# Attention block on one core: the last stage moved into the attention loop, two token tiles to a job, inverse root on GpSimd

## What is computed

```python
h = layernorm(x) * (1 + ca) + sa
q, k, v = split(h @ W_attn)                      # 16 heads of 16
att = softmax(causal(q @ k.T / 4)) * decay       # decay is 0 beyond 512 tokens back
x = x + ga * ((att @ v) @ W_proj)
h = layernorm(x) * (1 + cb) + sb
x = x + gb * (h @ (W + lora_weight).T + b)
```

## Time and profile before

| | |
|---|---|
| median of 3 runs | 1557.8 us (1557.61 to 1559.09) |
| profiled execution | 1560.7 us, its span 1558.8 us |
| mean granted TensorE clock | 0.966 of 2.4 GHz |
| busy over the span | PE 1280.6, ACT 1311.0, DVE 996.6, POOL 52.4 us |
| attention, first product to last rescaling | 205.9 to 1471.2 us |
| last stage, first load to the end of the span | 1474.7 to 1558.8 us |

### The profile page before, as it was taken

The page is one execution under the profiler, slowest core; times in us unless marked ns, Lnnn a source line. Parts: engine busy times, 40 slices in busy tenths (PEclk is TensorE's granted clock), DMA queues, the critical chain, the costliest instruction groups (busy, mean ns, idle before and its releaser), DMA issues. The chain is left out here.

```text
span 1558.8 us, 28424 instructions
## 1 busy us (share of the span) xinstructions
PE 1280.6 (82%) x11067; PEld 737.5 (47%) x11067; DVE 996.6 (64%) x2026; ACT 1311.0 (84%) x2677; POOL 52.4 (3%) x28
## 2 busy tenths in 40 slices
PE   7876168888888888888888888888888888777598
PEld 5543034545454545444445444554544444333387
DVE  4632147777777777777777777777776666554376
ACT  2533069999999999999999999999999999999532
POOL 0322000000000000000000000000000000000022
PEclk9988579999999999999999999999999999999799
DMA  4999970101010101010100000000101000100153
GB/s 149 203 218 198 169 97 1 35 1 35 2 35 1 35 1 29 7 35 2 27 10 17 20 13 23 11 26 8 25 6 27 9 23 10 23 4 4 37 168 128
DMA packets 111723, 72.96 MB, mean 47 GB/s; under 512 B 56395, under 2 KB 110946, under 8 KB 111586
## 3 DMA queue, kind: packets, MB, share of 16 engines
q1 hardware_dynamic: 111586, 71.13, 21.3%
HBM read 45.93 MB, written 25.17 MB: 46 GB/s over the span
## 5 line engine op out<-in xcount | busy, mean ns | idle before, releaser
L808 PE MATMUL fast_s_ps<-k_stack,fast_q_stack 96*128 96x512 bf16 (+3 forms) x2448 | 651.9, 354 | 178.2 <-ACT fast_probs L927 98.7
L927 ACT ACTIVATE fast_s_ps<-fast_s_ps,fast_negmax 128x1024 f32<-128x1024 f32 (+4 forms) x768 | 792.8, 1039 | 4.4 <-PE fast_s_ps L808 3.9
L949 DVE TENSOR_REDUCE fast_negmax<-fast_s_ps 128x1 f32<-128x640 f32 (+4 forms) x512 | 399.1, 780 | 134.5 <-PE fast_s_ps L811 130.0
L927 ACT ACTIVATE fast_probs<-fast_s_ps,fast_negmax 128x640 f32<-128x640 f32 (+7 forms) x512 | 436.6, 853 | 43.3 <-DVE fast_negmax L949 38.7
L958 DVE TENSOR_TENSOR fast_probsT<-fast_t_ps,fast_dec_c 128x384 f32<-128x384 f32 (+2 forms) x512 | 276.6, 540 | 197.1 <-PE fast_t_ps L826 197.1
L808 PEld LDWEIGHTS fast_s_ps<-k_stack,fast_q_stack 96*128 96x128 bf16 x2448 | 180.0, 97 | 451.2 <-ACT fast_s_ps L927 178.0
L826 PE MATMUL fast_t_ps<-ident,fast_probs 128*128 128x128 f32 x1488 | 250.2, 275 | 22.7 <-DVE fast_y_sb L989 20.8
L968 DVE TENSOR_TENSOR fast_probsT<-fast_t_ps,fast_dec_c 128x256 f32<-128x256 f32 x464 | 191.6, 413 | 66.9 <-PE fast_t_ps L842 66.9
L826 PEld LDWEIGHTS fast_t_ps<-ident,fast_probs 128*128 128x128 f32 x1488 | 172.4, 141 | 76.2 <-DVE fast_y_sb L989 27.9
L842 PE MATMUL fast_t_ps<-ident,fast_probs 128*128 128x128 f32 x912 | 187.2, 286 | 1.9
L857 PE MATMUL fast_t_ps<-fast_probsT,fast_vals 128*16 128x128 f32 x4800 | 180.9, 276 | 7.1 <-DVE fast_probsT L968 5.9
(11 more groups left out here) (107 smaller groups left out, 588.1 us busy)
## 6 DMA issues: line engine op xcount, KB each, us to landing
parts_d<-part SPq DMA_DIRECT2D x48, 256.0 KB, 12.5
k_stack<-parts_d SPq DMA_DIRECT2D x48, 256.0 KB, 9.7
fast_q_stack<-parts_d SPq DMA_DIRECT2D x192, 64.0 KB, 3.0
fast_vals<-v_d SPq DMA_DIRECT2D x36, 128.0 KB, 3.0
xs<-x_dram SPq DMA_DIRECT2D x8, 512.0 KB, 8.6
v_d<-w SPq DMA_DIRECT2D x8, 512.0 KB, 8.6
y_d<-fast_y_sb SPq DMA_DIRECT2D x32, 128.0 KB, 2.5
yy<-y_d SPq DMA_DIRECT2D x16, 256.0 KB, 2.7
```

The source lines that it names most:

```text
L808: last = nc.tensor.matmul(s_ps[:, n % SLOTS, o:o + w], q, k_stack[:, h, P * b0 + o:P * b0 + o + w], start=True, stop=not diag)
L927: nc.scalar.activation(dst, src, ACT.Exp, bias=negmax[:, p % 2, side, h:h + 1], scale=-1.0, accum_out=sums[:, p % 2, side, h, c:c + 1]).th ...
L949: nc.vector.tensor_reduce(out=negmax[:, p % 2, side, h:h + 1], in_=s_ps[:, n % SLOTS, max(0, cols - P * WIN):cols], axis=AX_X, op=ALU.min) ...
```

## The change

The last stage is taken out of its place behind the attention (it stays as `rest_full`, called only behind `attention_full`) and is done inside `attention_fast`, pair by pair. Both tiles of a finished pair make one job of 512 columns on bank two of `t_ps`, behind FAR's turn in steps h = 5 (turn of y), 7 (product with `wp_g`), 11 (turn of the normalised rows) and 13 (product with `wf_g`) of the next pair; for the last pair they follow behind the loop. In such steps fill 4 stands ahead of FAR's tail, as it did in group steps. VectorE takes over ScalarE's two copies; row statistics come in h = 8, the aggregates in h = 9. GpSimd computes 1/sqrt(var + eps) with an integer first guess and four Newton steps, 11 small operations a tile, each waiting for the one before, then normalises and adds the bias. q is loaded in halves of 8 heads, and y no longer goes to HBM.

```diff
+            HEAD_JOBS = {1: ("back", FAR), 3: ("back", NEAR)}
+            BOTH = 2
+            TAIL_JOBS = {5: ("y_turn", BOTH), 7: ("project", BOTH), 11: ("n_turn", BOTH), 13: ("linear", BOTH)}
...
-                q_stack = sb("fast_q_stack", [SROWS, 2, 2, NH, P], bf16, s2)
+                q_stack = sb("fast_q_stack", [SROWS, 2, 2, QH, P], bf16, s2)
...
+                    for u in range(2 * NPAIR):
+                        p = u // 2
+                        if u + 2 < 2 * NPAIR:
+                            sp.wait_ge(s_full, PER * QH * (u + 1))
+                            load_q(u + 2)
+                        if u % 2 == 0 and 0 < p < NPAIR - 1:
+                            sp.wait_ge(tail_full, tail_no["group", NEAR, NG4 * p - 1] + 1)
+                            load_vals(p + 1)
+                        if u % 2 == 1 and p > 0:
+                            store(p - 1)
+                            if p + 1 < NPAIR:
+                                sp.wait_ge(result_stored[(p - 1) % 2], 32 * ((p - 1) // 2 + 1))
+                                load_x(p + 1)
...
+                    def y_turn(p):
+                        pe.wait_ge(tail_free, tail_no["y_turn", BOTH, p])
+                        pe.wait_ge(turn_free, turn_no["back", NEAR, p] + 1)
+                        for side in (FAR, NEAR):
+                            for cc in range(CH):
+                                o = P * (CH * side + cc)
+                                last = nc.tensor.transpose(tail_ps[:, o:o + P], y_sb[:, side, P * cc:P * (cc + 1)], ident[:])
+                        last.then_inc(tail_full, 1)
+                    def through(weights, job):
+                        pe.wait_ge(tail_free, tail_no[job])
+                        for side in (FAR, NEAR):
+                            for cc in range(CH):
+                                last = nc.tensor.matmul(tail_ps[:, C * side:C * (side + 1)], tT[:, side, cc, :], weights[:, cc, :],
+                                                        start=(cc == 0), stop=(cc == CH - 1))
+                        last.then_inc(tail_full, 1)
+                    def n_turn(p):
+                        pe.wait_ge(norm_ready, 2 * p + 2)
...
                         turn(FAR, s)
                         if group_after(s):
                             values(*group_after(s), 1)
+                            fill(s, 4)
+                            turn_tail(FAR, s)
+                        elif job_after(s, TAIL_JOBS):
+                            tail_job(*job_after(s, TAIL_JOBS))
                             fill(s, 4)
                             turn_tail(FAR, s)
...
+                    def inverse_root(side):
+                        v, half, y, w = (b[:, side:side + 1] for b in (var_e, var_h, rstd, root_t))
+                        chained(nc.gpsimd.tensor_scalar(v, mv2[:, side, 1:2], EPS, None, ALU.add))
+                        chained(nc.gpsimd.tensor_scalar(half, v, -0.5, None, ALU.mult))
+                        chained(nc.gpsimd.tensor_scalar(y.bitcast(mybir.dt.int32), v.bitcast(mybir.dt.int32),
+                                                        -0.5, 1597463007.0, ALU.mult, ALU.add))
+                        for _ in range(4):
+                            chained(nc.gpsimd.tensor_scalar(w, y, y, half, ALU.mult, ALU.mult))
+                            chained(nc.gpsimd.tensor_scalar(y, w, three_halves[:, 0:1], y, ALU.add, ALU.mult))
+                    for p in range(NPAIR):
+                        for side in (FAR, NEAR):
+                            pool.wait_ge(stats_done, 2 * p + side + 1)
+                            inverse_root(side)
+                            x2 = xb[:, p % 2, side, :]
+                            nc.gpsimd.tensor_scalar(y_sb[:, side, :], x2, mv2[:, side, 0:1], rstd[:, side:side + 1],
+                                                    ALU.subtract, ALU.mult).then_inc(norm_ready, 1)
+                            pool.wait_ge(norm_ready, 2 * p + side + 1)
+                            nc.gpsimd.tensor_tensor(x2, x2, f_bias[:], ALU.add).then_inc(bias_added, 1)
...
+                    def row_sums(h, p):
+                        if h == 8:
+                            spread(FAR, p)
+                            spread(NEAR, p)
+                        if h == 9:
+                            statistics(FAR, p)
+                            statistics(NEAR, p)
```

More of the change, by code:

```diff
@@ L710, in attention_fast @@
                 next_tail("group", side, NSTEP // HG - 1)
-            for side in (FAR, NEAR):
-                next_turn("back", side, NPAIR - 1)
+            for kind, side in HEAD_JOBS.values():
+                next_turn(kind, side, NPAIR - 1)
+            for kind, side in TAIL_JOBS.values():
+                next_tail(kind, side, NPAIR - 1)
             s2 = ExitStack()
@@ L761, in _, with load_q @@
                 def _(sp):
-                    def load(p):
+                    def load_q(u):
+                        p, half = u // 2, u % 2
                         for side in (FAR, NEAR):
@@ L774, in store @@
                     def store(p):
                         for side in (FAR, NEAR):
[L776 to L784, removed]
-                            sp.wait_ge(tail_full, tail_no["group", NEAR, NG4 * p - 1] + 1)
-                            load(p + 1)
-                        store(p - 1)
+                            sp.wait_ge(tail_free, tail_no["linear", BOTH, p] + 1)
@@ L869, in turn_back, with head_job, tail_job @@
                         last.then_inc(turn_full, 1)
+                    def y_turn(p):
[15 more added lines that the diff above has]
+                        pe.wait_ge(norm_ready, 2 * p + 2)
+                        pe.wait_ge(tail_free, tail_no["n_turn", BOTH, p])
+                        for side in (FAR, NEAR):
+                            for cc in range(CH):
+                                o = P * (CH * side + cc)
+                                last = nc.tensor.transpose(tail_ps[:, o:o + P], y_sb[:, side, P * cc:P * (cc + 1)], ident[:])
+                        last.then_inc(tail_full, 1)
+                    def head_job(kind, side, p):
+                        turn_back(side, p)
+                    def tail_job(kind, side, p):
+                        if kind == "y_turn":
+                            y_turn(p)
+                        elif kind == "project":
+                            through(wp_g, (kind, side, p))
+                        elif kind == "n_turn":
+                            n_turn(p)
+                        else:
+                            through(wf_g, (kind, side, p))
                     pe.wait_ge(k_last, 16 * len(PAIRS))
@@ new lines, in result, with head_job @@
+                    def result(p):
+                        dve.wait_ge(tail_full, tail_no["linear", BOTH, p] + 1)
+                        dve.wait_ge(bias_added, 2 * p + 2)
+                        x2 = xb[:, p % 2]
+                        nc.vector.tensor_tensor(x2, x2, tail_ps.rearrange("p (s c) -> p s c", s=2), ALU.add).then_inc(tail_free, 1)
+                    def head_job(kind, side, p):
+                        if side == FAR:
+                            factors(p)
+                        finish(side, p)
@@ L1015, in _ @@
                     group_to_sb(NEAR, NSTEP // HG - 1)
-                    factors(NPAIR - 1)
-                    finish(NPAIR - 1, FAR)
-                    finish(NPAIR - 1, NEAR)
+                    for h in range(NH):
+                        row_sums(h, NPAIR - 1)
+                        if h in HEAD_JOBS:
+                            head_job(*HEAD_JOBS[h], NPAIR - 1)
+                        if h in TAIL_JOBS:
+                            tail_job(*TAIL_JOBS[h], NPAIR - 1)
                     nc.vector.tensor_reduce(out=worst_row[:], in_=worst[:], axis=mybir.AxisListType.XY, op=ALU.max
@@ L1660 @@
+            rest_full()
 def kernel(**inputs):
```

527 lines of the change are left out of this document (298 added, 229 removed).

## The result

The changed kernel takes **1618.4 us** (median of 4 runs, 1617.07 to 1621.29), the kernel before 1558.4 (4 runs, 1557.61 to 1568.1): ratio 1.0373, 95% interval 1.0329 to 1.0416. It is slower by 3.7%; the forecast was 1545.8 with a range to 1581, so the time lies outside it. The cause is rival A, larger than I had priced it.

The account below looks back on a forecast made before the run. ScalarE's exponentials were taken to bound the attention (97% busy). From a span of 1558.8 us, 59.2 saved at the end, 50.6 given back inside the attention and 3.4 saved at the start made 12.0 less: 1545.8 us, range 1526 to 1581.

Parts of the forecast that it names:

- rival A: GpSimd late for the turn of n at h = 11, TensorE and ScalarE waiting: 1582 us at c = 0.45; chance 0.20.
- GpSimd's chain: Inverse root, normalisation and bias of both tiles, between h = 9 and 11: 9.0 us in 9.7 available, cost 0.
- T: Time of GpSimd's work on a pair's two tiles, 22c + 0.5 + 0.75 + 0.5 + 0.2, predicted 9.0 us.
- c: Time of one small chained GpSimd operation: taken as 0.32 us between bounds 0.24 and 0.40; stops fitting at 0.355.
- Large jobs: Product and add in h = 7 and 13 of 15 pairs: each step loses 1.41 us on average.
- Rival B: Jobs in the attention better hidden by ScalarE's three slots: 21 us given back instead of 50.6, 1516 us; chance 0.13.
- Small jobs: Turn and copy in h = 5 and 11 of 15 pairs: each step loses 0.28 us on average.
- Rival C: Delay carries into the even step behind each job: 60 x 0.42 = 25 us more, 1571 us; chance 0.11.
- Row statistics: VectorE's statistics in h = 8 and h = 9 fall into its idle time: 0; without that cover up to 12 us.
- The start: Loading q in halves starts the attention's first product earlier: 3.4 us saved, bounds 0 and 9.
- The old stage's clock: The stage behind the attention, 87.6 us removed, was said to run its 16 batches of 4.33 us at full clock.
- The end: Last pair's jobs run alone after the last rescaling, ending at 1499.6 instead of 1558.8: 59.2 us saved.

Follow-up runs that it names:

- experiment 6: Changed kernel with the inverse root for both tiles at once, no pointer operands, still four Newton steps, 19 operations instead of 22: 1554.0 us, ratio 0.9943 to the kernel before.
- experiment 1: Changed kernel with two Newton steps on GpSimd instead of four: 1558.4 us, ratio 0.9974 to the kernel before.
- experiment 5: Changed kernel with 20 throwaway transposes on TensorE ahead of its wait for the normalised rows, in all pairs but the last: 1598.7 us, ratio 1.0235.
- experiment 3: Changed kernel with the turn of the normalised rows at h = 13 and the product behind it at h = 15: 1558.75 us, ratio 0.9970.
- experiment 10: Kernel before with q loaded in halves of eight heads and nothing else of the change: 1558.5 us, ratio 0.9961.
- experiment 7: Changed kernel with the inverse root moved to VectorE in h = 9, normalisation and bias staying on GpSimd: 1648.1 us, ratio 1.0548.
- experiment 2: Changed kernel with three Newton steps on GpSimd instead of four: 1571.4 us, ratio 1.0041 to the kernel before.
- experiment 4: Changed kernel with the turn of the normalised rows at h = 13 and six Newton steps instead of four: 1562.4 us, ratio 0.9995.

## Why the prediction was wrong

- **GpSimd's chain, the step that failed.** The rule was right: late by T less 9.7. T was mis-sized: 22c + 0.5 + 0.75 + 0.5 + 0.2 = 9.0, measured 12.4. Of the 3.4 us, 2 x 0.75 = 1.5 are the normalisation (0.5 taken, 1.25 measured), which I had costed as "one input less" and not bounded at all; 22 x (0.41 - 0.32) = 1.9 are the small operations. c lay just over the upper bound of 0.40, because of the pointers (experiment 6), which the prediction named as absent from every row of before and then left outside the bound. The normalisation itself, same size and same two pointers, did stand in the trace of before, on VectorE (L1646): 0.41 us, the median of 32 (experiment 6). The prediction did not use it. With 1.25 for each normalisation c would have had to stay under (9.7 - 3.45) / 22 = 0.284. The choice "T = 9.0 fits: 0" with 0.7 us to spare between bounds 3.5 us apart (22 x 0.16) was no forecast to give 0.56 to. The Trainium skill (GPSIMD Engine Reference, section 4.1) says that on GpSimd an operation with one input is "roughly line-rate" against VectorE; the trace does not bear this out for this form: the 128x256 one with one tensor input and two pointers takes 1.22 to 1.25 us on GpSimd, three times its 0.41 on VectorE, and more than GpSimd's two-input one of the same size (0.72).
- **Rival A's price.** With the measured T it gives 1546.8 + 15 x 2.65 + 3.4 = 1590 us of span; the span is 1617.4, 27 more. In the steps GpSimd's lateness costs 60 us (experiment 1) where this formula has 15 x 2.65 = 40; the clock, with 22 us in pairs 1 to 14 (experiment 5), more than fills that gap of 20. The rest is 3.5 for the jobs (54.1 against 50.6), the drain's other 1.8, and 1.3 in h = 3 of pair 13, where the clock fell too. The low clock stood in the rows, at the seam, where I used it for the drain; I did not ask what a wait of TensorE inside the attention would do to it.
- **Duration and spacing.** The Trainium skill (Perfetto Trace Analysis, GPSIMD Engine Instruction) advises timing GpSimd by start-to-start spacing. The trace agrees: a pointer operation shows 344 ns, and the next, which waits for it, starts 444 ns after it did.
- **Large jobs: right.** 1.41 us predicted, 1.41 measured at h = 7 and 13; by pair 1.34 in pair 1 (1.3 predicted), 1.60 in pair 7 (1.6), 1.82 in pair 15 (1.8). Counting through the step's chain, tried on the turning back at h = 3, holds. Rival B falls.
- **Small jobs:** 0.28 predicted, 0.14 measured (h = 5, and h = 13 in experiment 3: 0.15).
- **Rival C:** a carry-over into the next even step exists, at 0.09 to 0.12 us in h = 6, 8 and 14, not 0.42.
- **Row statistics,** costed at nothing: h = 9 is unchanged and h = 8 0.09 longer, in which the carry-over of h = 7 lies as well. Right.
- **The start:** 3.4 predicted, 3.1 measured in this profile; by experiment 10 closer to 6. Inside its bounds of 0 and 9.
- **The old stage's clock.** The prediction has its batches "all at full clock"; the clock was 0.50 until 1484, so the first product took 3.82 us. The 87.6 us removed do not rest on this.
- **The end:** 28.4 us predicted from the last rescaling, 33.5 measured: 3.4 are GpSimd's, and behind the result's add it is 7.2 against 5.4; what the stores take there I had read off the old stage's single one. To the start of GpSimd (7.5) and from the turn of n to the result (6.4) it is as predicted.

With T under 9.7 the sign of the forecast holds, and nearly its size: 1545.8 is 0.9923 of the kernel before; experiment 6 gives 0.9943 (0.9920 to 0.9965), experiments 1 and 3 0.9974 and 0.9970. Of these only 3 has a longer end (32.7 us from the last rescaling, against 28.5 in 6 and 28.7 in 1); from the first exponential on, the profiles of 1 and 6 are equally long (1347.9 us), so what divides their ratios is open.

Open: whether the two pointers alone make the 128x256 normalisation cost 1.25 us (an immediate form of that size was not run), and why two half jobs lose 0.27 us each rather than the 0.15 of a small job.

## What to carry to other kernels

Where a step is put on an idle engine, compare its latency, not its load, with the time to its consumer, and ask for a margin as wide as the uncertainty of that latency; if the operand forms of the chain stand in no row, the bound has to be wider than the rows. Batch a chain of small operations over the tiles and keep pointer operands out of it, or move the consumer to a later step: either takes away all that GpSimd's lateness cost in the steps. A wait that stops TensorE costs more than its own length once its clock falls, so price a rival that makes it wait with the low clock behind it.

## What was not expected of the hardware

- An operand from a pointer: 0.444 us from start to start in place of 0.27 to 0.31 on GpSimd, 0.31 in place of 0.19 on VectorE (operations with one or two elements per partition, each waiting for the one before).
- GpSimd's 128x256 operation with two pointers at 1.25 us, beside 0.72 for the addition of two tensors.
- In the attention the granted clock fell to 0.50 for 3.4 or 6.8 us at every wait of TensorE of 1.3 to 2.6 us for n, and for 6.8 us at every one of 3.6 to 4.7 us in experiment 7, there mostly while the wait still ran. At waits for n of 0.50 to 0.84 us (experiment 2) it stayed at 1.00, but at stands of about 1 us and less in h = 1 and 3 it sometimes fell.
- GpSimd's chain beside VectorE and ScalarE cost no time in h = 9 to 12 (experiments 3 and 4): steps of 4.71 and 4.95 us to the hundredth with and without it.
